# Additive attention in pieces of one token, 128 channels and 2048 rows, ahead of a quantised FFN

## What is computed

```python
features = _layernorm(x)
txt_proj = einsum('btd,de->bte', text, Ws)
feat_proj = einsum('bfd,de->bfe', features, W)
h = tanh(txt_proj[:, None, :, :] + feat_proj[:, :, None, :] + b)
rho = einsum('bftd,d->bft', h, w[:, 0]) + (1 - q_masks) * NEG
att = softmax(rho, axis=-1)
txt_h = einsum('bft,btd->bfd', att, text)
w_s = tanh(txt_h @ Wcw.T + bcw);  b_s = tanh(txt_h @ Wcb.T + bcb)
x = x + tanh(g_xattn) * (w_s * features + b_s)
x = x + tanh(g_ffn) * ffn(_layernorm(x))     # int8-like fake quantisation, silu(gate) * up, down
```

## Time and profile before

| | us |
|---|---|
| median of 3 runs | 1470.35 |
| lowest, highest of them | 1467.57, 1470.43 |
| the profiled execution, first to last instruction (span) | 1468.0 |
| ACT busy in it | 1279.5 (87%) |
| DVE busy in it | 1373.7 (94%) |
| PE busy in it | 1064.5 (73%) |
| POOL busy in it | 396.4 (27%) |

### The profile page before, as it was taken

The page is one execution under the profiler, slowest core; times in us unless marked ns, Lnnn a source line. Parts: engine busy times, 40 slices in busy tenths (PEclk is TensorE's granted clock), DMA queues, the critical chain, the costliest instruction groups (busy, mean ns, idle before and its releaser), DMA issues.

```text
span 1468.0 us, 23763 instructions
## 1 busy us (share of the span) xinstructions
PE 1064.5 (73%) x7531; PEld 402.7 (27%) x7531; DVE 1373.7 (94%) x3193; ACT 1279.5 (87%) x649; POOL 396.4 (27%) x181
## 2 busy tenths in 40 slices
PE   5676767676777677676767676767665559999897
PEld 3232213221322223122313231322111124444342
DVE  6999999999999999999999998999898758999888
ACT  1899999999999999999999998999899856665676
POOL 2011024424250444062422405241546500000000
PEclk9999999999999999999999999999889779999999
DMA  8000000000000000000000000000000013411286
GB/s 295 16 15 0 15 1 15 15 1 0 15 14 1 7 8 14 1 15 0 20 1 21 0 20 1 20 0 14 1 1 0 0 51 123 151 51 36 87 301 207
DMA packets 25754, 56.98 MB, mean 39 GB/s; under 512 B 2731, under 2 KB 2747, under 8 KB 25685
## 3 DMA queue, kind: packets, MB, share of 16 engines
q1 hardware_dynamic: 25365, 56.17, 11.3%
q0 software_dynamic: 320, 0.01, 0.0%
HBM read 42.01 MB, written 14.16 MB: 38 GB/s over the span
## 4 chain that ended last, share of the span: by engine, by line
ACT 34%; issue 25%; DVE 17%; PE 15%; POOL 4%; DMA 3%; DVEq 1%; ACTq 1%; SPq 0%; POOLq 0%
ACT big L397 27%; DVE big L637 11%; PE ps L1175 8%; POOL wst L361 4%; PE ps L1052 3%; DMA aux<-in_x_dram 3%; ACT big L418 2%; PE ps L1060 2%; ACT big L440 2%; PE ps L1011 1%; DMA big<-in_L_xattn_Ws_dram 1%; ACT aux L442 1%; DVE big L917 1%; ACT big L500 1%; DVE wgu L935 1%
## 5 line engine op out<-in xcount | busy, mean ns | idle before, releaser
L397 ACT ACTIVATE big<-big 128x4096 f32<-128x4096 f32 x274 | 969.1, 3614 | 43.6 <-DVE big L637 42.0
L637 DVE TENSOR_SCALAR big<-big,atxt 128x512 f32 (+1 forms) x2220 | 888.6, 478 | 12.7 <-PE ps L1052 12.0
L1052 PE MATMUL ps<-big,wst 128*32 128x512 f32 x4608 | 568.3, 615 | 313.1 <-ACT big L397 277.4
L361 POOL COPY wst<-wslide 128x128 f32 (+1 forms) x160 | 387.7, 2433 | 781.0 <-PE ps L1052 713.8
L1052 PEld LDWEIGHTS ps<-big,wst 128*32 128x32 f32 x4608 | 124.6, 111 | 649.4 <-ACT big L397 394.8
L1175 PE MATMUL ps<-aux,wgu 128*128 128x512 bf16 x680 | 151.7, 379 | 0.1
L981 PEld LDWEIGHTS ps<-aux 128*128 128x128 f32 x896 | 109.6, 193 | 95.5 <-issue 95.5
L981 PE MATMUL ps<-aux 128*128 128x128 f32 x896 | 131.0, 290 | 0.0
L487 ACT ACTIVATE aux<-ps,sgux 128x512 f32<-128x512 f32 x88 | 60.1, 686 | 58.9 <-PE ps L1175 54.0
L1193 PE MATMUL ps<-wd,wgu 128*128 128x512 bf16 x352 | 80.1, 385 | 9.2 <-DVE wgu L942 9.2
L1175 PEld LDWEIGHTS ps<-aux,wgu 128*128 128x128 bf16 x680 | 65.2, 98 | 73.8 <-DVE big L917 0.6
(11 more groups left out here) (144 smaller groups left out, 576.0 us busy)
## 6 DMA issues: line engine op xcount, KB each, us to landing
aux<-in_x_dram SPq DMA_DIRECT2D x64, 256.0 KB, 2.8
out_dram<-aux SPq DMA_DIRECT2D x32, 256.0 KB, 2.7
big<-in_x_dram SPq DMA_DIRECT2D x7, 1024.0 KB, 15.2
hidden_spill<-big SPq DMA_DIRECT2D x6, 768.0 KB, 5.6
big<-hidden_spill SPq DMA_DIRECT2D x6, 768.0 KB, 6.2
aux<-in_L_ffn_w_gate_dram SPq DMA_DIRECT2D x11, 256.0 KB, 2.6
aux<-in_L_ffn_w_up_dram SPq DMA_DIRECT2D x11, 256.0 KB, 3.0
aux<-in_L_ffn_w_down_dram SPq DMA_DIRECT2D x4, 704.0 KB, 4.1
```

What stands on the lines that cost most here:

```text
L361: nc.gpsimd.tensor_copy(wst[:, slot, :, :], wslide[:, :, bass.ds(g * (-1) + 31, 32)]).then_inc(wst_ready, 1)
L397: nc.scalar.activation(th[:, slot, :, :, :], th[:, slot, :, :, :], ACT.Tanh).then_inc(tanh_done, 1)
L637: last = v.tensor_scalar(th[:, slot, j, e, :].rearrange("p (t c) -> p t c", t=BTL), xf[:, bass.ds(BTL * q, BTL), ch * P:(ch + 1) * P], atx ...
L1052: last = mm(bank(SCORE)[32 * j:32 * j + 32, :], wst[:, wslot, 2 * half + e, :], th[:, slot, j, e, :], start=False, stop=True, skip_group_c ...
```

## The change

The attention is laid out anew; the FFN stays. The work is now cut into 616 pieces of one token x 128 channels x 2048 rows (`PIECES` = 2 batches x 4 chunks x 77 tokens), phase after phase: all 77 tokens of one chunk of one batch, then the next chunk. A ring of 8 pieces (`RING`) is used in two halves of four (`UNIT`, `NSLOT`). VectorE adds the text column to the whole 2048 columns of a piece in one instruction (`add_text`), ScalarE applies tanh to a half of the ring, 4 pieces or 8192 columns, in one instruction, and TensorE scores a piece with four products of 512 columns (`score`), whose stationary operand is a slice of the sliding buffer `wslide` itself; GpSimd's copies are gone. An add into a slot of the ring waits until the piece that was 8 earlier has been scored; a score waits for the tanh of its half. All loops are written out. The scores of a batch lie in three PSUM banks, and there is one softmax per batch in place of one per block.

The first 8 pieces are made by ScalarE with the text column as bias (`early_tanh`), 512 rows at a time, while the rows of batch 0 are still being normalised. Batch 0 is normalised in three groups of 4, 4 and 8 tiles before the first add. The rows of batch 1 are loaded twice, once for their statistics and once to be normalised, while the attention of batch 0 runs. A phase's features are projected during the phase before it (`FEAT_AT`, 4 parts of 512 rows), on TensorE ahead of the score of the piece named there, and copied by VectorE 9 pieces later (`LAG`). The 15 weight jobs, the row maxima, the statistics and the softmax of batch 0 each stand ahead of the add of the piece that a table names.

```diff
-    C4 = 4
-    TG = -(-T // C4)
-    UNITS = 2 * (TG - 2) + 1 + EC
+    PIECES = B * EC * T
+    PER_B = EC * T
+    UNIT, NSLOT = 4, 2
+    RING = UNIT * NSLOT
+    NUNIT = -(-PIECES // UNIT)
+    EARLY = 2 * UNIT
+    KG = -(-T // 32)
+    Q4 = 4
...
+        LAG = RING + 1
+        MAX0_AT = {8 + 2 * i: i for i in range(BT)}
+        STATS_AT = {84 + 4 * i: i for i in range(BT)}
+        CHAIN_AT = 150
+        NORM_AT = {172 + 7 * i: i for i in range(BT)}
+        MAX1_AT = {at + 2: i for at, i in NORM_AT.items()}
+        COPY_AT = {at + LAG: i for at, i in NORM_AT.items()}
+        FEAT_AT = {}
+        for ph in range(1, B * EC):
+            first = (ph - 1) * T
+            turns = {3: (2, 4, 14, 16), 4: (14, 16, 30, 58)}.get(ph, (24, 26, 38, 40))
+            for part in range(Q4):
+                FEAT_AT[first + turns[part]] = (ph, part)
+        FEAT_COPY_AT = {at + LAG: f for at, f in FEAT_AT.items()}
+        QUANT_AT = dict(zip((50, 64, 80, 96, 112, 128, 200, 220, 262, 365, 378, 400, 445, 475, 522), range(NJOB)))
+        WT_AT = {at + 1: j for at, j in QUANT_AT.items()}
+        WCOPY_AT = {at + 1 + LAG: j for at, j in QUANT_AT.items()}
+        RHO_AT = PER_B + RING
+        SHIFT_AT = {PER_B + 14 + UNIT * c: c for c in range(Q4)}
+        EXP_AFTER = {at // UNIT + 2: c for at, c in SHIFT_AT.items()}
+        SUMS_AT = {at + 24: c for at, c in SHIFT_AT.items()}
...
-            def stationaries(g, slot):
-                nc.gpsimd.tensor_copy(wst[:, slot, :, :], wslide[:, :, bass.ds(g * (-1) + 31, 32)]).then_inc(wst_ready, 1)
...
+            def early_tanh(part):
+                act.wait_ge(feat_ready, part + 1)
+                act.wait_ge(atxt_ready, 1)
+                cols = slice(part * 512, (part + 1) * 512)
+                for t in range(EARLY):
+                    last = nc.scalar.activation(ring[:, t, cols], feat[:, 0, cols], ACT.Tanh, bias=atxt[:, 0, t:t + 1])
+                    if part == Q4 - 1 and t % UNIT == UNIT - 1:
+                        last.then_inc(tanh_done, 1)
...
+            for u in range(EARLY // UNIT, NUNIT):
+                n = min(UNIT, PIECES - u * UNIT)
+                at = UNIT * (u % NSLOT)
+                act.wait_ge(sums_ready, u * UNIT + n - EARLY)
+                nc.scalar.activation(ring[:, at:at + n, :], ring[:, at:at + n, :], ACT.Tanh).then_inc(tanh_done, 1)
+                if u in EXP_AFTER:
+                    exp_scores(0, EXP_AFTER[u])
...
+            def add_text(p):
+                ph, t = p // T, p % T
+                bt, e = ph // EC, ph % EC
+                if p >= RING:
+                    dve.wait_ge(scored, p - RING + 1)
+                v.tensor_scalar(ring[:, p % RING, :], feat[:, ph % 2, :], atxt[:, e, bt * T + t:bt * T + t + 1], None,
+                                ALU.add).then_inc(sums_ready, 1)
...
+            def project(ph, part):
+                n, e = Q4 * ph + part, ph % EC
+                pe.wait_ge(xnT_ready, BT * (ph // EC) + 4 * (part + 1))
+                if n >= 2:
+                    pe.wait_ge(feat_ready, n - 1)
                 for k in range(EC):
+                    last = mm(bank(FB[n % 2]), w_sb[:, k, e * P:(e + 1) * P], xnT[:, k, part * 512:(part + 1) * 512],
+                              start=(k == 0), stop=(k == EC - 1))
+                last.then_inc(projected, 1)
...
+            def score(p):
+                e, t = p // T % EC, p % T
+                k, g = t // 32, t % 32
+                if p % UNIT == 0:
+                    pe.wait_ge(tanh_done, p // UNIT + 1)
+                for part in range(Q4):
+                    last = mm(bank(k)[32 * part:32 * part + 32, :], wslide[:, e, 31 - g:63 - g],
+                              ring[:, p % RING, part * 512:(part + 1) * 512], start=(e == 0 and g == 0), stop=True,
                               skip_group_check=True)
                 last.then_inc(scored, 1)
...
+            for p in range(PIECES):
...
+                if p in FEAT_AT:
+                    ph, part = FEAT_AT[p]
...
+                    project(ph, part)
+                if p in WT_AT:
+                    transpose_weights(WT_AT[p])
...
+                score(p)
```

## The result

| | before | after |
|---|---|---|
| median, us | 1470.39 | 1581.05 |
| lowest, highest of the runs | 1467.57, 1470.93 | 1579.78, 1583.55 |
| ratio to before, 95% interval | | 1.076 (1.075 to 1.078) |
| span of the profiled execution | 1468.0 | 1580.1 |
| granted clock of TensorE over the span | 0.969 | 0.865 |

A forecast was written before the change was run, and what follows sets the result against it. ScalarE's tanh bounds the attention: start 62, tanh 1052, projections 44 and VectorE's other work 52 make 1210; with 22 and 273 for the end 1505; with 75 for TensorE's clock 1580, median 1583; range 1497 to 1615.

The forecast's parts named there:

- The prices: Attention: tanh of 8192 columns 7.02 us alone, 6.91 back to back; adds of 2048 columns 1.29 and 1.21.
- Rival (d): VectorE's adds in the attention take 2.0 us each, making about 1735 us in all; chance 0.04.
- The start and the end: First large tanh at 62 us, give or take 5; 22 us after the last tanh, then 273 to the end.
- 44, 52, 75 and 2 for the exponentials: Attention: us added for projections, VectorE's other work, TensorE's falling clock, and four exponentials on ScalarE.
- The projections: TensorE, ahead of scores: free before a unit's first score, 2.4 to 1.7 us before later ones; 44 us in all.
- The clock: TensorE's clock falls in long waits in every second unit, 1.0 us each: 75 us, bounds nothing and 258.
- the price of a fall: TensorE's scores after long waits in the old last block: two clock falls cost 1.7 and 3.0 us.
- VectorE's steps: Weight jobs, statistics, softmax sums and small steps on VectorE make ScalarE wait 52 us together.
- rival (a): TensorE's clock stays up in the attention: 1508 us; chance 0.15.
- (b): TensorE's clock stays down for most scores: 1766 us; chance 0.05.
- Rival (c): ScalarE never waits, projections and VectorE's steps hide in VectorE's idle time, and the clock holds: 1412 us; chance 0.10.

The follow-up runs named there:

- the kernel with all three edits: Changed kernel with projections and VectorE's steps moved to the starts of units, plus zero products on TensorE after a unit's fourth score: 1460.41 us (0.995).
- with the order mended: Changed kernel with projections and VectorE's steps at the starts of units: 1517.01 us without added zero products on TensorE, 1460.41 us with them.
- a filler that leaves out the units with projections: Changed kernel plus 12 zero products on TensorE after a unit's fourth score, except where a projection or batch end follows: 1540.83 us (1.049).

## Why the prediction was right

**The prices** held. Tanh of 8192 columns takes 7.03 us alone and 6.92 back to back (7.02 and 6.91 forecast), an add of 2048 columns 1.28 alone and (4.88 - 1.28) / 3 = 1.20 behind another (1.29 and 1.21). Rival (d), adds of 2.0 us that keep VectorE busy throughout, is gone with the adds' length and with the 329 us that VectorE waits.

**The start and the end** (first large tanh, last one, and the end of the softmax, in the timeline of ScalarE):

```profile
63.42 13.95 ACT L424 ACTIVATE big<-big 128x8192 f32<-128x8192 f32 x2 [5.07 <-DVE big L612]
...
1277.52 7.03 ACT L424 ACTIVATE big<-big 128x8192 f32<-128x8192 f32 x1 [0.76 <-DVE big L612]
...
1307.32 0.53 ACT L431 ACTIVATE gate_ws<-soft,scal 128x32 f32<-128x32 f32 x2 [9.68 <-DVE soft L764]
```

The first large tanh stands at 63.4 us, against 35.2 in the earlier trace rows and 62 forecast. From the last one's end at 1284.55 to the end of L431 at 1307.85 are 23.3 us (22 forecast, 10.2 in the earlier trace rows), and from there to the end 272.2 (273). The two ends are 41 us longer than in the kernel before. Against this stand the 8 pieces that ScalarE has made before the first large tanh, some 14 us of the old attention (an estimate: 4 times the 3.51 us of 4096 columns).

**Between them** lie 1221 us, 72 more than the 1149 of the kernel before. ScalarE waits there 162.9 - 5.1 = 158 us; the stretch from 63.42 to 1284.55 is 169 us longer than 152 tanh of 6.92 us each, where 44, 52, 75 and 2 for the exponentials had been summed up, 173. I sorted the waits ahead of each tanh by what the tables of the change put into its refill: 17 units with a projection between those scores wait 61 us, 15 with a weight job 31, 58 with other steps of VectorE 53, and the 61 with none of these 14.

**The single terms** are less exact than their sum. The projections are worth 53 us (44 forecast). The next score starts 3.63 us after a part (251.27 to 254.90), not 3.43, which is 4 us for the 20 parts inside units; what the other 5 us are stays open. It is not the clock in the parts, for 25 of the 28 take 3.70 us, as they do in the kernel with all three edits at 0.99. The clock is worth 57 us with the order mended and 40 by a filler that leaves out the units with projections (75 forecast): the rows of the last block gave the price of a fall, but how many falls meet a unit that is late already was a guess. VectorE's steps come close to the forecast 52: moving some of them takes away 12 us of waits, and in the kernel with all three edits, where the clock and the projections no longer count, 39 us are left, 15 of them ahead of units with a weight job and 23 with other steps. So the clock was put too high and the projections too low, and the terms act on each other (121 us together, 103 one by one). That the sum came within 2 us is partly luck; by its own terms it gives 1580 + 2.3 = 1582 and not 1583. What holds is the mechanism: three kinds of lateness, each moved by an edit of its own.

**The clock as a mechanism.** It stayed neither up, as in rival (a), nor down, as in (b): slow and fast scores take turns, and over the attention it is 0.84. In 80 units the trace has the 32 instructions of the scores as one group with nothing between; 43 of these groups took 5.0 to 6.6 us and the others 3.64, about every second one, as forecast. A slow group ends later and so shortens the next wait. The Trainium skill ("TensorE: Matmul & The Clock Gate", section "Loop structure matters more than you think") calls a loop bad in which a long wait for a DMA stands ahead of every matmul, which then runs cold. The waits here are for ScalarE; the trace agrees for 3.65 and 4.46 us, after which the scores took 6.47 and 5.34, while after 0.45 and 1.58 they took 3.64. That the length of the wait alone decides is not shown, since the shorter waits of the four parts come with shorter scores.

**Rival (c)**, that ScalarE never waits, became true of another layout of the same ring: with four parts of two pieces it waits 6.3 us, and the time is 1424 where (c) had 1412. What spoke against it, that VectorE's free time lies at one place of the unit only, is what the smaller parts change.

## What to carry to other kernels

In a ring that several engines pass on, count the parts and not only the columns: the room for a step that comes in addition is the time that ScalarE spends on the other parts, minus the refill of one. With two halves that was 0.7 us. With four parts it is some 6.7 us (an estimate: three tanh of 3.51, minus 0.1, minus a refill of 3.7, which is a score of 1.06, two hand-overs of 0.07 as in the prediction, and two adds of 2.48). Work that has nothing to do with the ring costs less ahead of a unit than inside (weight jobs 1.6 us against 2.7, the projections 53 us in all), so its place counts as well as its size. Larger instructions save the fixed cost of the ones they replace (28 us of tanh for 304 instructions, from one piece to two), but they make the bursts and the waits of the engine behind them longer, and here TensorE's clock fell in them.

## What the runs showed of the hardware

TensorE's clock is an effect and a cause: 383 us of products with zeros made a kernel 40 us faster. With four parts, waits of 1.58 us between scores of 1.92 go with a clock of 0.99 over 1050 us. With two halves the same products come in scores of 3.64 us at the upper level, with waits of up to 4.46 us in the timeline shown, and the clock is 0.84.

ScalarE's tanh takes 1.80, 3.51 and 6.92 us for 2048, 4096 and 8192 columns back to back, which is 0.83 ns for each further column and 0.1 us for an instruction. The Trainium skill ("ScalarE: Activation LUTs", section "Rules for kernel authors") advises to budget about 0.3 us for an instruction whose bias is read from a pointer operand, and 0.83 ns for an element. The trace agrees on the second, and on the first for the tanh with such a bias: 0.716 us for 512 columns, of which 0.29 is not columns. The large tanh has no such operand, and its instructions follow each other; there it is 0.1.
